# Attention projections from fp16 halves made by GpSimd, with the score scale moved into the queries' flips

## The chip, the core and the metric

The kernel runs as one program on one core of a Trainium2 chip. The metric is the device time of one execution in microseconds (us). The core's engines are PE (TensorE, matrix products; its weight loads are listed as PEld), DVE (VectorE), ACT (ScalarE), POOL (GpSimd) and the DMA queues, which SP (SyncE) and POOL issue to. Each engine runs its own list of instructions in order; they meet at semaphores.

## The reference, cut to what matters

One transformer block over x of 4 batches x 512 tokens x 128 channels: a normalisation with scale and shift, attention, a second normalisation, a mixture of eight experts. The part of attention that the change touches:

```
q = (x @ wq).reshape(B, N, H, D)       # B=4, N=512, H=16 heads, D=64
k = (x @ wk)                           # KV=4 heads, repeated to 16
v = (x @ wv)                           # KV=4 heads, repeated to 16
for n in range(K_NODES):               # 4 nodes; a token belongs to its top 2
    p = pos[..., n]                    # position of the token within node n
    qr = q * cos[p] + rotate_half(q) * sin[p]
    kr = k * cos[p] + rotate_half(k) * sin[p]
    scores = einsum('bhid,bhjd->bhij', qr, kr) * D ** -0.5
    scores = where(causal & member, scores, NEG)
    outs.append(einsum('bhij,bhjd->bhid', softmax(scores), v))
y = (tk_w * take(outs, tk_idx)).sum()
out = y @ wo
```

Everything is float32 in the reference.

## The kernel before, in words

The order of every engine's work is written out by hand. First comes a **preamble** (up to about 69 us): loads, first normalisation, `hT` (the normalised tokens, channels on the partitions, 128 x 2048), router scores, the choice of nodes and positions, and the first sines and cosines. Then comes the **attention loop**: 64 heads (4 batches x 16), numbered `n`, four steps `s` each (one block of 128 query rows), so k = 4n + s runs over 256 steps. Then comes the expert part with the output.

In the preamble SP loads the weights `wq` and `wk` into `w_qk` and `wv` into `w_v`; ACT multiplies the query weights by 0.125, which is the score scale (L557). DVE does the long chain that chooses nodes and positions (L807 to L894), POOL makes constants and two casts (L393).

For each head:
- `project(n)` on PE (L1184): four matmuls of float32, one for each block of 128 tokens, with 128 columns (64 of q, 64 of k), into the PSUM bank `psM`. `project_value(g)` (L1177) does four of 64 columns once for every four heads.
- `products(n, e)` on DVE (L905) multiplies them by cosines and sines, `rotate(n, part)` on POOL (L410 to L429) adds them up into `R` (queries in both slots) and `ktok`.
- `flip(i)` on PE turns a block of 128 tokens around: two transposes for the queries (L1228) and one for the keys (L1230), each through `ident`, a float32 identity. ACT copies the three results from PSUM to `QK` (L596, `keep_qk`).
- `scores(k)` on PE (L1243 to L1248), row maxima on DVE (L933, L940), exponentials on ACT (L617), coefficients on POOL (L436), the two weighted sums on ACT (L626) and DVE (L951), `prob_rows` on PE (L1257, one to four transposes), `values` (L1268) and every eight heads `attention_rows` (L1293).

PE's order in step k is: scores(k), flip(k+2), prob_rows(k-4), and in some steps values, project_value, attention_rows; in step s = 3 project(n+3) ends the step. A flip or prob_rows needs one of three PSUM banks in turn, so it waits until ACT has emptied the one used three turns before. DVE also makes the angles for later heads (L850 to L878) inside the loop, and once in eight heads ACT turns them into sines and cosines (L579, L580, with two table loads). POOL splits the experts' weights into float16 halves in step s = 1 of 48 heads (L449, L451).

## Time and profile before

| what | value |
|---|---|
| median of 3 runs | 980.61 us (980.22 to 987.98) |
| the profiled execution, its own time | 980.4 us |
| span from its first to its last instruction | 978.6 us |
| PE busy | 860.6 us, 88% of the span |
| DVE, ACT, POOL busy | 80%, 77%, 65% of the span |
| TensorE clock granted, mean | 0.965 of full speed |

The span is divided by reading the trace in stretches: the preamble ends with the first scores at 68.83 us, and the attention loop ends at 845.6 us. A profile's busy time of PE includes the modelled tail of each matmul, so the cost of one in a row of them is read from start to start. A float32 matmul appears in the trace as two instructions (x8 for the four of `project`), a float32 transpose and a float16 matmul as one.

### The profile page before, as it was taken

How to read it: one execution, taken by the hardware profiler on the slowest of the kernel's cores; microseconds unless marked ns; L12 is line 12 of the kernel's file. 1: busy time of each engine (PE TensorE's matmuls, PEld its weight loads, DVE VectorE, ACT ScalarE, POOL GpSimd, SP SyncE). 2: the span in 40 equal slices, each digit the busy share in tenths (PEclk: the TensorE clock that was granted, in tenths of full speed). 3: DMA queues.
4: the chain of work that ended last, by engine and by line, in shares of the span. 5: the costliest groups of instructions: out<-in, count | busy, mean ns of one | idle time of the engine just before them, and what ended most of it. 6: DMA issues, size and time to landing. Idle time of an engine off the chain costs nothing.

```text
span 978.6 us, 19653 instructions
## 1 busy us (share of the span) xinstructions
PE 860.6 (88%) x5960; PEld 610.1 (62%) x5960; DVE 787.0 (80%) x1832; ACT 753.6 (77%) x2032; POOL 632.5 (65%) x898
## 2 busy tenths in 40 slices
PE   4348979998999899989998999899989999998883
PEld 4336656666666665666666666666667676665773
DVE  4979979996999699969996999689967876686554
ACT  8427888788888888888788888888888887764552
POOL 1157767885878588857885788577856665036562
PEclk9659999999999999999999999999999999999997
DMA  9000001000100000100010000000000000324443
GB/s 223 13 0 8 13 12 33 26 24 12 28 29 27 11 24 27 32 13 23 24 34 13 24 24 28 20 24 24 19 2 2 3 2 10 111 76 135 116 127 103
DMA packets 54279, 36.65 MB, mean 37 GB/s; under 512 B 8384, under 2 KB 53056, under 8 KB 54176
## 3 DMA queue, kind: packets, MB, share of 16 engines
q1 hardware_dynamic: 52960, 32.88, 12.4%
q0 software_dynamic: 1216, 2.51, 0.8%
q8 instruction: 51, 0.84, 0.4%
q14 instruction: 52, 0.43, 0.1%
HBM read 22.23 MB, written 12.36 MB: 35 GB/s over the span
## 4 chain that ended last, share of the span: by engine, by line
PE 60%; DVE 26%; ACT 7%; issue 5%; POOL 1%; DMA 1%; DVEq 0%; ACTq 0%; POOLq 0%; SPq 0%
PE psum L1243 21%; PE psum L1268 7%; PE psum L1257 6%; PE psum L1184 5%; DVE pcs L905 4%; PE psum L1351 4%; PE psum L1228 4%; PE psum L1248 4%; DVE accs L951 3%; ACT probs L617 3%; DVE psum L940 3%; PE psum L1293 3%; DVE probs L1002 2%; DVE arena L878 2%; PE psum L1230 2%
## 5 line engine op out<-in xcount | busy, mean ns | idle before, releaser
L1243 PE MATMUL psum<-QK 128*128 128x128 f32 (+3 forms) x1024 | 375.4, 452 | 1.3 <-ACT QK L596 1.3
L617 ACT ACTIVATE probs<-psum,negmax 128x128 f32<-128x128 f32 (+3 forms) x512 | 266.5, 527 | 80.0 <-DVE negmax L940 48.1
L410 POOL TENSOR_TENSOR R<-pcs 128x512 f32<-128x512 f32 x128 | 190.5, 1509 | 64.9 <-DVE pcs L905 47.3
L940 DVE CUSTOM_DVE_ANT_0 psum<-psum,causal 128x384 f32<-128x384 f32 (+1 forms) x256 | 156.4, 637 | 57.8 <-PE psum L1248 57.6
L436 POOL TENSOR_TENSOR coef<-rden,wslot 128x2 f32<-128x2 f32 x256 | 87.2, 340 | 171.2 <-DVE rden L946 171.1
L1243 PEld LDWEIGHTS psum<-QK 128*128 128x128 f32 x1024 | 166.7, 195 | 45.7 <-issue 40.9
L951 DVE SCALAR_TENSOR_TENSOR accs<-probs,coef,accs 128x128 f32<-128x128 f32 (+3 forms) x256 | 169.2, 661 | 1.0 <-ACT accs L626 1.0
L626 ACT ACTIVATE accs<-probs,coef 128x128 f32<-128x128 f32 (+3 forms) x256 | 148.0, 578 | 23.3 <-POOL coef L436 23.3
L905 DVE TENSOR_TENSOR pcs<-psum,arena 128x512 f32<-128x512 f32 x256 | 161.7, 672 | 0.0
L1257 PE MATMUL psum<-ident,accs 128*128 128x128 f32 x640 | 116.3, 280 | 38.2 <-ACT QK L596 34.3
L596 ACT ACTIVATE QK<-psum 128x384 f32<-128x384 f32 x256 | 125.8, 491 | 1.9 <-PE psum L1230 1.8
L933 DVE TENSOR_REDUCE negmax<-psum 128x2 f32<-128x256 f32 (+1 forms) x128 | 70.5, 550 | 61.0 <-PE psum L1246 60.7
L605 ACT ACTIVATE arena<-psum 128x128 f32<-128x128 f32 (+3 forms) x256 | 114.6, 448 | 0.0
L1257 PEld LDWEIGHTS psum<-ident,accs 128*128 128x128 f32 x640 | 72.0, 141 | 62.9 <-issue 41.5
L617 ACT ACTIVATION_READ_ACCUMULATOR probs<-psum,negmax 128x1 f32 x512 | 102.8, 201 | 0.0
L1228 PE MATMUL psum<-ident,R 128*128 128x128 f32 x512 | 101.0, 279 | 1.3
L1184 PE MATMUL psum<-w_qk,hT 128*128 128x128 f32 x512 | 74.1, 291 | 30.1 <-DVE pcs L905 25.2
L1228 PEld LDWEIGHTS psum<-ident,R 128*128 128x128 f32 x512 | 59.7, 143 | 52.2 <-issue 42.0
L1248 PE MATMUL psum<-mring 128*128 128x384 f16 (+1 forms) x256 | 90.2, 352 | 0.0
L1184 PEld LDWEIGHTS psum<-w_qk,hT 128*128 128x128 f32 x512 | 67.0, 204 | 32.0 <-issue 18.9
L1268 PE MATMUL psum<-arena,v_b 128*64 128x256 f32 (+3 forms) x512 | 76.0, 439 | 0.9 <-ACT arena L605 0.7
L1230 PE MATMUL psum<-ident,ktoks 128*128 128x128 f32 x256 | 70.6, 276 | 0.0
(214 smaller groups left out, 1469.3 us busy)
## 6 DMA issues: line engine op xcount, KB each, us to landing
weight_halves<-whl SPq DMA_DIRECT2D x48, 128.0 KB, 2.2
arena<-weight_halves SPq DMA_DIRECT2D x22, 256.0 KB, 3.2
arena<-weight_halves SPq DMA_DIRECT2D x7, 512.0 KB, 6.9
wst<-in_L_ffn_w_up_dram SPq DMA_DIRECT2D x14, 128.0 KB, 2.5
wst<-in_L_ffn_w_gate_dram SPq DMA_DIRECT2D x14, 128.0 KB, 2.4
wst<-in_L_ffn_w_down_dram SPq DMA_DIRECT2D x14, 128.0 KB, 2.5
sorted_rows<-arena SPq DMA_DIRECT2D x1, 1430.0 KB, 11.4
QK<-sorted_rows SPq DMA_DIRECT2D x5, 260.0 KB, 3.9
```

Of the source, the lines that this page charges most:

```text
L410: pool.tensor_tensor(R[u][:, :, :, 0:3:2, half * HALF:(half + 1) * HALF].rearrange("p t e j f -> p (t e) j f"), halves(pc, half), halves(p ...
L617: act.activation((expB if e else expA)[:, k % (4 if e else 3), 0:w], area, ACT.Exp, scale=1.0 if k % TB < 2 else -1.0, bias=negmax[k % 4][ ...
L626: act.activation(acc[k % 4][:, 0:w], expA[:, k % 3, 0:w], ACT.Copy, scale=coef[k % 4][:, 0:1]).then_inc(S["wa_done"], 1)
L905: dve.tensor_tensor(dst[:, :, e, :].rearrange("p t (j f) -> p t j f", f=HALF), src, table.unsqueeze(2).to_broadcast([P, TB, 4, HALF]), ALU ...
L940: dve.tensor_tensor_reduce(score_area(k, e), score_area(k, e), causal[:, T - w:T], -1.0, 3e38, ALU.add, ALU.min, accum_out=negmax[k % 4][: ...
L951: dve.scalar_tensor_tensor(acc[k % 4][:, 0:w], expB[:, k % 4, 0:w], coef[k % 4][:, 1:2], acc[k % 4][:, 0:w], ALU.mult, ALU.add).then_inc(S ...
L1184: mm_ = pe.matmul(psM[:, tb * P:(tb + 1) * P], hT[:, b * T + tb * P:b * T + (tb + 1) * P], w_qk[:, h, :, :].rearrange("p j d -> p (j d)"), ...
L1228: pe.transpose(psT[:, e * P:(e + 1) * P], R[u][:, tb, e, 0:2, :].rearrange("p c d -> p (c d)"), ident[:, :])
L1243: pe.matmul(o, QK[:, u, e, rows], QK[:, u, 2, 0:w], start=True, stop=False)
L1248: mm_ = pe.matmul(o, mring[:, r, 1 + e, rows], mring[:, r, 0, 0:w], start=False, stop=True)
L1257: mm_ = pe.transpose(psPT[:, jb * P:(jb + 1) * P], acc[k % 4][:, jb * P:(jb + 1) * P], ident[:, :])
L1268: mm_ = pe.matmul(dst[u * HD:(u + 1) * HD, jb * P:T], v_b[:, p // 2 % 3, jb, :], accT[:, (2 * p + u) % 3, jb, jb * P:T], start=(jb == 0), ...
```

## The change

Attention's projections are made of float16 halves. A float32 value is kept as high = fp16(value) and low = fp16(value - high), and a product is the sum of three float16 matmuls (high x high, high x low, low x high) accumulated in PSUM. The helper `three`, which the expert part already has, is moved ahead and used in `project` and `project_value`. The weights `wq`, `wk`, `wv` are loaded as float32 into a part of `probs` that is still free; POOL splits them into `w_qk` and `w_v` (now float16, high and low), and then the tokens of batch 0 into a buffer that the router uses later. The tokens of batches 1 to 3 are split in the loop, 128 columns at a time, in step s = 3 of the heads n = 4 to 15, into the place of the `hT` of the batch before. PE waits for the halves (`hs_lo`). The query weights are no longer scaled. Instead the two query transposes of `flip` become plain float32 matmuls with `ident_q`, an identity times 0.125. The column of gates `gcol` is made by a copy instead of a multiplication with `ones`.

```
@@ -59,7 +59,7 @@
         ones16 = sb("ones16", [P, P], F16)
-        ones = sb("ones", [P, P])
+        ident_q = sb("ident_q", [P, P])
         half_pi = sb("half_pi", [P, 1])
@@ -71,8 +71,8 @@
-        w_qk = sb("w_qk", [P, H, 2, HD])
-        w_v = sb("w_v", [P, KV * HD])
+        w_qk = sb("w_qk", [P, 2, H, 2 * HD], F16)
+        w_v = sb("w_v", [P, 2, KV * HD], F16)
         w_r = sb("w_r", [P, H * NODES])
@@ -146,6 +146,9 @@
         w_mod = probs[:, :, :].rearrange("p g t -> p (g t)")[:, 0:6 * DIM]
+        w_qk32 = probs[:, :, :].rearrange("p g t -> p (g t)")[:, 1024:1024 + H * 2 * HD]
+        w_qk4 = w_qk32.rearrange("p (h j d) -> p h j d", j=2, d=HD)
+        w_v32 = probs[:, :, :].rearrange("p g t -> p (g t)")[:, 3072:3072 + KV * HD]
         xn = pcs_flat.rearrange("p (t d) -> p t d", d=DIM)
@@ -193,15 +196,20 @@
         passed = red_flat[:, 168:168 + SORTED * (E - 1)].rearrange("p (t e) -> p t e", e=E - 1)
-        rl = sb("rl", [P, NT, E])
-        rr = sb("rr", [P, 4, NT, E])
+        rbuf = sb("rbuf", [P, 4 * NT * E])
+        rl = rbuf[:, 0:NT * E].rearrange("p (t e) -> p t e", e=E)
+        rr = rbuf[:, NT * E:4 * NT * E].rearrange("p (k t e) -> p k t e", k=3, e=E)
         rm = sb("rm", [P, 4, NT])
-        one16 = rr[:, 3, :, :].rearrange("p t e -> p (t e)").bitcast(F16)[:, 0:(NT + 1) * E].rearrange(
-            "p (t e) -> p t e", e=E)
+        one16 = sb("one16", [P, NT + 1, E], F16)
+
+        def halves_of(b):
+
+            where = rbuf[:, 0:T] if b == 0 else hT[:, (b - 1) * T:b * T]
+            return where.bitcast(F16).rearrange("p (l t) -> p l t", l=2)
...
             mm_in0 mm_in1 mm_in2 c_exp c_sum c_rec c_silu mod_mm mod_raw mod_sign mod_mag mod_done
-            gcol_done ga_mm ga_ev wq_scaled bn_s bn_a var_e std_dev rs_step xn_done xn_a xn_t h_ready zeros_done big_done
+            gcol_done ga_mm ga_ev hs_hi hs_lo bn_s bn_a var_e std_dev rs_step xn_done xn_a xn_t h_ready zeros_done big_done
             lg_mm lg_ev rank_s rank_m w_tanh l_mem mem16 sel_a sel_b sel_cp code_p code_e gap_done
@@ -276,11 +284,11 @@
             sp.dma_start(w_r[:, :], wr).then_inc(S["wr_in"], 16)
-            sp.dma_start(w_qk[:, :, 0, :], wq.rearrange("p (h d) -> p h d", h=H)).then_inc(S["wr_in"], 16)
+            sp.dma_start(w_qk4[:, :, 0, :], wq.rearrange("p (h d) -> p h d", h=H)).then_inc(S["wr_in"], 16)
             for r in range(GROUP):
-                sp.dma_start(w_qk[:, r:H:GROUP, 1, :], wk.rearrange("p (g d) -> p g d", g=KV)
+                sp.dma_start(w_qk4[:, r:H:GROUP, 1, :], wk.rearrange("p (g d) -> p g d", g=KV)
                              ).then_inc(S["loaded"], 16)
-            for dst, src in ((freq[:, :], inv_freq), (w_v[:, :], wv),
+            for dst, src in ((freq[:, :], inv_freq), (w_v32, wv),
                              (w_o[:, :, :], wo.rearrange("(c p) n -> p c n", p=P)), (w_rt[:, :], w_router)):
@@ -359,12 +367,12 @@
             for t_, v in ((one_half, 0.5), (ident, 0.0), (ident16, 0.0), (identbig, 0.0), (causal, 0.0), (before, 1.0),
-                          (ones16, 1.0), (ones, 1.0), (half_pi, float(np.pi / 2))):
+                          (ones16, 1.0), (ident_q, 0.0), (half_pi, float(np.pi / 2))):
                 pool.memset(t_[:, :], v).then_inc(S["const_done"], 1)
...
             pool.wait_ge(S["const_done"], 11)
-            for t_, v in ((ident, 1.0), (ident16, 1.0), (identbig, BIG)):
+            for t_, v in ((ident, 1.0), (ident_q, HD ** -0.5), (ident16, 1.0), (identbig, BIG)):
                 pool.affine_select(out=t_[:, :], in_=t_[:, :], compare_op=ALU.not_equal, fill=v, base=0,
@@ -386,6 +394,19 @@
             pool.memset(floor8[:, E - 1:E], float(SORTED * P)).then_inc(S["ident_done"], 1)
+            def split_rows(i, high, low, src):
+                pool.tensor_copy(high, src).then_inc(S["hs_hi"], 1)
+                pool.wait_ge(S["hs_hi"], i + 1)
+                pool.tensor_tensor(low, src, high, ALU.subtract).then_inc(S["hs_lo"], 1)
+
+            pool.wait_ge(S["wr_in"], 32)
+            pool.wait_ge(S["loaded"], 16 * 8)
+            w_two = w_qk[:, :, :, :].rearrange("p l h c -> p l (h c)")
+            split_rows(0, w_two[:, 0, :], w_two[:, 1, :], w_qk32)
+            split_rows(1, w_v[:, 0, :], w_v[:, 1, :], w_v32)
+            pool.wait_ge(S["h_ready"], 1)
+            split_rows(2, halves_of(0)[:, 0, :], halves_of(0)[:, 1, :], hT[:, 0:T])
+            pool.wait_ge(S["lg_mm"], 2)
             pool.wait_ge(S["sel_a"], 4)
@@ -454,6 +475,10 @@
                     split(n - RING - 1)
+
+                if s == 3 and 4 <= n < 4 + (B - 1) * TB:
+                    b, cols = (n - 4) // TB + 1, slice((n - 4) % TB * P, (n - 4) % TB * P + P)
+                    split_rows(n - 1, halves_of(b)[:, 0, cols], halves_of(b)[:, 1, cols], hT[:, b * T:(b + 1) * T][:, cols])
                 m, part = (n + 2, s - 2) if s >= 2 else (n + 1, s + 2)
@@ -553,8 +578,6 @@
                 act.activation(lg[:, i * 512:(i + 1) * 512], bank[4 + i][:, :], ACT.Copy).then_inc(S["lg_ev"], 1)
-            act.wait_ge(S["wr_in"], 32)
-            act.activation(w_qk[:, :, 0, :], w_qk[:, :, 0, :], ACT.Copy, scale=HD ** -0.5).then_inc(S["wq_scaled"], 1)
             act.preload_act_table(ACT.Silu)
@@ -779,7 +802,7 @@
             dve.wait_ge(S["mod_raw"], 1)
-            dve.wait_ge(S["ident_done"], 7)
+            dve.wait_ge(S["ident_done"], 8)
             for j in range(2):
@@ -796,7 +819,7 @@
             for b in range(B):
-                dve.tensor_scalar(gcol[b], ones[:, :], mod[:, 2, b:b + 1], None, ALU.mult).then_inc(S["gcol_done"], 1)
+                dve.tensor_copy(gcol[b], mod[:, 2, b:b + 1].to_broadcast([P, P])).then_inc(S["gcol_done"], 1)
@@ -1141,7 +1164,7 @@
             mm_.then_inc(S["mod_mm"], 1)
-            pe.wait_ge(S["ident_done"], 7)
+            pe.wait_ge(S["ident_done"], 8)
@@ -1171,18 +1194,27 @@
+            def three(dst, w, x_, start, stop):
+                for j, (wl, xl) in enumerate(((0, 0), (0, 1), (1, 0))):
+                    mm_ = pe.matmul(dst, w[wl], x_[xl], start=start and j == 0, stop=stop and j == 2)
+                return mm_
+
+            def rows_of(b, tb):
+                return [halves_of(b)[:, l, tb * P:(tb + 1) * P] for l in range(2)]
+
             def project_value(g):
                 b = g // KV
+                pe.wait_ge(S["hs_lo"], 3 + TB * b)
                 for tb in range(TB):
-                    mm_ = pe.matmul(psM[:, tb * HD:(tb + 1) * HD], hT[:, b * T + tb * P:b * T + (tb + 1) * P],
-                                    w_v[:, (g % KV) * HD:(g % KV + 1) * HD], start=True, stop=True)
+                    mm_ = three(psM[:, tb * HD:(tb + 1) * HD], rows_of(b, tb),
+                                [w_v[:, l, (g % KV) * HD:(g % KV + 1) * HD] for l in range(2)], True, True)
                 mm_.then_inc(S["v_mm"], 1)
...
                 b, h = n // H, n % H
+                pe.wait_ge(S["hs_lo"], 3 + TB * b)
                 for tb in range(TB):
-                    mm_ = pe.matmul(psM[:, tb * P:(tb + 1) * P], hT[:, b * T + tb * P:b * T + (tb + 1) * P],
-                                    w_qk[:, h, :, :].rearrange("p j d -> p (j d)"), start=True, stop=True)
+                    mm_ = three(psM[:, tb * P:(tb + 1) * P], rows_of(b, tb), [w_qk[:, l, h, :] for l in range(2)], True, True)
                 mm_.then_inc(S["qk_mm"], 1)
@@ -1197,7 +1229,6 @@
                 mm_.then_inc(S["pos_mm"], 1)
-            pe.wait_ge(S["wq_scaled"], 1)
             pe.wait_ge(S["v_ev"], 1)
@@ -1225,8 +1256,9 @@
                 for e in range(2):
-                    pe.transpose(psT[:, e * P:(e + 1) * P], R[u][:, tb, e, 0:2, :].rearrange("p c d -> p (c d)"),
-                                 ident[:, :])
+
+                    pe.matmul(psT[:, e * P:(e + 1) * P], R[u][:, tb, e, 0:2, :].rearrange("p c d -> p (c d)"),
+                              ident_q[:, :], start=True, stop=True)
                 pe.transpose(psT[:, 2 * P:3 * P], ktok[u][:, tb, :, :].rearrange("p c d -> p (c d)"), ident[:, :]
@@ -1345,11 +1377,6 @@
                 mm_.then_inc(S["rank_mm"], 1)
-
-            def three(dst, w, x_, start, stop):
-                for j, (wl, xl) in enumerate(((0, 0), (0, 1), (1, 0))):
-                    mm_ = pe.matmul(dst, w[wl], x_[xl], start=start and j == 0, stop=stop and j == 2)
-                return mm_
...
                 if i >= 2:
```

**PE, the last projection of the preamble and the first flips**, before (`R` holds queries, `ktoks` keys):

```order
L1184 MATMUL psum<-w_qk,hT 128x128 [waits prod_done]
L1184 MATMUL psum<-w_qk,hT 128x128 x3
L1228 MATMUL psum<-ident,R 128x128 [waits k_done,q_done]
L1228 MATMUL psum<-ident,R 128x128
L1230 MATMUL psum<-ident,ktoks 128x128
L1228 MATMUL psum<-ident,R 128x128 [waits k_done,q_done]
L1228 MATMUL psum<-ident,R 128x128
L1230 MATMUL psum<-ident,ktoks 128x128
```

and in the changed kernel (`rbuf` holds the halves of batch 0's tokens):

```order
L1199 MATMUL psum<-w_qk,rbuf 128x128 [waits hs_lo,prod_done]
L1199 MATMUL psum<-w_qk,rbuf 128x128 x11
L1260 MATMUL psum<-ident_q,R 128x128 [waits k_done,q_done]
L1260 MATMUL psum<-ident_q,R 128x128
L1262 MATMUL psum<-ident,ktoks 128x128
L1260 MATMUL psum<-ident_q,R 128x128 [waits k_done,q_done]
L1260 MATMUL psum<-ident_q,R 128x128
L1262 MATMUL psum<-ident,ktoks 128x128
```

Each projection has 12 float16 matmuls where it had 4 of float32, with a wait on the halves; the flips stand where they stood, and two of the three are matmuls now.

**POOL, end of the constants to the first rotation**, before:

```order
L383 IOTA arena 128x22 [waits zeros_done,const_done]
L386 AFFINE_SELECT tri<-tri 128x64
L388 MEMSET floor 128x1
L393 CAST QK<-yT 128x1024 [waits sel_a]
L393 CAST QK<-yT 128x1024 [waits sel_b]
L410 TENSOR_TENSOR R<-pcs 128x8x2x32 [waits prod_done,codes_done]
```

and in the changed kernel:

```order
L391 IOTA arena 128x22 [waits zeros_done,const_done]
L394 AFFINE_SELECT tri<-tri 128x64
L396 MEMSET floor 128x1
L398 CAST w_qk<-probs 128x2048 [waits loaded,wr_in]
L400 TENSOR_TENSOR w_qk<-probs,w_qk 128x2048 [waits hs_hi]
L398 CAST w_v<-probs 128x256
L400 TENSOR_TENSOR w_v<-probs,w_v 128x256 [waits hs_hi]
L398 CAST rbuf<-hT 128x512 [waits h_ready]
L400 TENSOR_TENSOR rbuf<-hT,rbuf 128x512 [waits hs_hi]
L414 CAST QK<-yT 128x1024 [waits sel_a,lg_mm]
L414 CAST QK<-yT 128x1024 [waits sel_b]
L431 TENSOR_TENSOR R<-pcs 128x8x2x32 [waits prod_done,codes_done]
```

Six splitting instructions stand ahead of the two casts `QK<-yT`, for which PE waits (`sel_cp`).

**POOL, around step s = 3 of head n = 4** (`coef` are the coefficients that ACT waits for, `R` the next head's rotation), before:

```order
L410 TENSOR_TENSOR R<-pcs 128x8x2x32 [waits t_done,prod_done]
L410 TENSOR_TENSOR R<-pcs 128x8x2x32
L436 TENSOR_TENSOR coef<-rden,wslot 128x2 [waits rden_done]
L415 TENSOR_TENSOR R<-R,code 128x8x64 [waits add_done]
L418 TENSOR_TENSOR kdif<-R 128x256
L436 TENSOR_TENSOR coef<-rden,wslot 128x2 [waits rden_done]
```

and in the changed kernel:

```order
L431 TENSOR_TENSOR R<-pcs 128x8x2x32 [waits t_done,prod_done]
L431 TENSOR_TENSOR R<-pcs 128x8x2x32
L457 TENSOR_TENSOR coef<-rden,wslot 128x2 [waits rden_done]
L398 CAST hT<-hT 128x128
L400 TENSOR_TENSOR hT<-hT 128x128 [waits hs_hi]
L436 TENSOR_TENSOR R<-R,code 128x8x64 [waits add_done]
L439 TENSOR_TENSOR kdif<-R 128x256
L457 TENSOR_TENSOR coef<-rden,wslot 128x2 [waits rden_done]
```

A cast and a subtraction of 128 columns stand ahead of the second part of the next rotation and the coefficients after it; this occurs 12 times, in heads 4 to 15.

## Rows read from the trace of the kernel before

**Rows 1.** The chain that ended last, of the attention loop, by line.

```profile
by line: PE psum L1243 26.7%; PE psum L1268 8.9%; PE psum L1257 7.6%; PE psum L1184 5.7%; PE psum L1228 4.7%; DVE pcs L905 4.6%; PE psum L1248 4.4%; DVE accs L951 4.2%; ACT probs L617 4.2%; DVE psum L940 4.0%; issue 3.6%; PE psum L1293 3.2%
```

**Rows 2.** Busy us of eight heads on PE, PEld, DVE, ACT, POOL; then clock, DMA.

```profile
264.21:362.95 98.74, 93.61 (x578) 64.53 (x577) 84.62 (x194) 82.80 (x236) 73.91 (x105) 0.98 0.08 24
```

**Rows 3.** Timeline of PE at full clock: start us, us, line.

```profile
407.86 0.38 PE L1228 MATMUL psum<-ident,R 128*128 128x128 f32 x2
408.07 0.27 PE L1230 MATMUL psum<-ident,ktoks 128*128 128x128 f32 x1
408.18 0.60 PE L1257 MATMUL psum<-ident,accs 128*128 128x128 f32 x4
408.62 1.06 PE L1184 MATMUL psum<-w_qk,hT 128*128 128x128 f32 x8
409.51 0.39 PE L1243 MATMUL psum<-QK 128*128 128x128 f32 x2
```

**Rows 4.** The groups of PE by shape: busy us, mean ns of one.

```profile
L1169 PE MATMUL psum<-ident,kdif 128*128 128x128 f32 x4 | 0.7, 288 | 0.0
```

**Rows 5.** The chain of 264 to 363 us, in order of time: start, us, what.

```profile
271.68 2.14 DVE arena L878
...
274.60 1.45 ACT probs L617 x4
...
278.75 0.41 PE psum L1257 x2
...
346.25 0.84 PE psum L1177 x8
```

**Rows 6.** The waits of the whole span: us in total, times, longest us.

```profile
PE psum L1257 <- ACT QK L596: 34.3, 33, 3.5
```

**Rows 7.** Timeline of PE in the expert part: float16 matmuls in a row.

```profile
906.31 1.50 PE L1351 MATMUL psum<-mk,arena 128*128 128x128 f16 x24
907.65 0.90 PE L1397 MATMUL psum<-ident,QK 128*128 128x128 f32 x6
```

**Rows 8.** The chain of the preamble, in order of time.

```profile
22.94 3.25 DVE arena L807 x6
...
65.54 2.07 PE psum L1184 x8
67.61 0.43 PE psum L1228 x2
```

**Rows 9.** DMA issues: KB each, median us from issue to landing.

```profile
w_rt<-in_L_ffn_w_router_dram SPq DMA_DIRECT2D x1, 4.0 KB, 4.4
```

**Rows 10.** The groups of POOL by shape: busy us, mean ns of one.

```profile
L451 POOL TENSOR_TENSOR whl<-wst,whl 128x256 f16<-128x256 f32 x48 | 32.3, 673 | 3.8
L449 POOL CAST whl<-wst 128x256 f16<-128x256 f32 x48 | 19.0, 396 | 0.0
```

**Rows 11.** Timeline of the preamble: last load, PE, POOL's casts, DVE's angles.

```profile
11.96 0.58 SPq L285 DMA_DIRECT2D w_rt<-in_L_ffn_w_router_dram  x1
...
31.09 0.21 PE L1196 MATMUL psum<-arena,before 128*128 128x64 f16 x1 [3.25 <-DVE arena L819]
...
32.85 3.07 POOL L393 CAST QK<-yT 128x1024 f16<-128x1024 f32 x2 [21.05 <-DVE yT L827]
...
38.91 1.29 DVE L850 TENSOR_TENSOR arena<-slot,freq 128x512 f32<-128x512 f32 x2
...
42.82 0.46 DVE L873 TENSOR_SCALAR arena<-arena 128x576 f32<-128x576 f32 x1
...
53.35 2.34 DVE L850 TENSOR_TENSOR arena<-slot,freq 128x512 f32<-128x512 f32 x2
...
60.67 0.76 DVE L873 TENSOR_SCALAR arena<-arena 128x576 f32<-128x576 f32 x1
```

**Rows 12.** Busy us and timeline of PE after a long wait.

```profile
325.90:329.20 3.30, 3.30 (x17) 3.17 (x18) 0.00 (x0) 2.16 (x7) 0.00 (x0) 0.50 0.00 0
...
325.87 2.04 PE L1184 MATMUL psum<-w_qk,hT 128*128 128x128 f32 x8 [0.51 <-DVE x L963]
```

## The prediction

> **What bounds the kernel now.** I read the chain of waits of the attention loop first, by line, then the busy times of eight heads, then PE's timeline from start to start. The chain [rows 1] is mostly PE's: of the loop's 776.8 us (68.83 to 845.6) the score products L1243 have 26.7%, the projections L1184 5.7% and the query flips L1228 4.7%; DVE and ACT lines have the smaller pieces. In eight heads PE is busy 93.61 of 98.74 us, DVE 84.62, ACT 82.80, POOL 73.91 [rows 2]. So PE is the nearest bound and DVE the next. The expert part from 845.6 us on keeps its instructions; I cost it at nothing.
>
> **The flips, the largest term.** At full clock two query transposes take 0.21 us from start to start (407.86 to 408.07), the key's takes 0.11 and four of L1257 take 0.44, so a float32 transpose costs 0.11 us. The four float32 matmuls of a projection take 0.89 us (408.62 to 409.51), so a matmul of the same shape costs 0.2225 [rows 3]. The change turns 512 transposes (64 heads x 4 blocks x 2) into such matmuls: 512 x 0.1125 = 57.6 us more work for PE. That an identity as second operand makes nothing cheaper is seen at L1169, two plain matmuls by `ident`, which the trace has as four instructions [rows 4].
>
> A page speaks of another ratio. The Trainium skill (TensorE: Matmul & The Clock Gate, Terms) says that transpose mode is four times faster for float32. The rows just named give a factor of two, and I go by them; what four would do is the last rival.
>
> Not all of this is on the path. The chain's share of L1228 is 4.7% of 776.8 = 36.5 us, which is 329 transposes of 0.111. The others lie beside DVE or ACT work: the chain of one stretch goes through an angle step of DVE (2.14 us), then four instructions of ACT's exponentials (1.45 us), and comes back to PE at 278.75 [rows 5]. PE waited 34.3 us in 33 such places for ACT's copy, up to 3.5 us each [rows 6]; the two or three flips in front of such a place add only 0.23 us each, and vanish in it. So on the path: 329 x 0.1125 = **+37.0 us**, as a floor; if no wait hid anything, 57.6.
>
> **The projections.** A float16 matmul of 128 columns takes (907.65 - 906.31) / 24 = 0.056 us [rows 7]. Three of them, 0.168, replace 0.2225: 0.0545 saved x 256 = 14.0 us of PE work, 24.5% of L1184. The chain has 5.7% of 776.8 = 44.3 us of that line [rows 1]; 24.5% of it is **-10.9 us**. The 16 value projections (64 columns) took 0.84 us for eight instructions [rows 5], 0.21 a matmul. The trace has no float16 one of this shape in a steady row; at 0.168 for three, like the wider one, it saves 0.042 x 64 = 2.7, at half that time 8. I take **-2.0**, since the wide one has the same weight load, and keep 0 and -8.
>
> **The flips that are hidden now.** These floors hold if every wait stays as long as it is. Some waits are shorter than what is put in front of them, and there the flip becomes the later one. Of the 57.6 - 37.0 = 20.6 us that lie beside other work I let a tenth come through: **+2.0**, bounds 0 and 20.6.
>
> **The preamble.** The last projection before the loop is on the chain at half clock: 2.07 us, of which 65.54 to 67.61 is its length; the first two flips take 0.43 us each for their pair [rows 8]. The projection gets shorter by a quarter, -0.5, the two flips by 0.43 longer each, +0.9: **+0.4**. ACT's scaling of the query weights goes; it stood beside the chain of DVE, which runs without a hole from 22.94 us, so it gives nothing.
>
> POOL's splitting is new there. It starts when the last load has landed: `w_rt` is issued at 11.96 [rows 11] and takes 4.4 us [rows 9], so 16.4. The work per 256 columns is 0.396 for the cast and 0.673 for the subtraction [rows 10]. The query and key weights are 2048 columns: 8 x (0.396 + 0.673) = 8.6; the value weights 1.1; the tokens of batch 0 (512) 2.1. In all 11.8 us, to 28.2. Queued behind it are the two casts that POOL began at 32.85 us before, when DVE's selection is there [rows 11]; 4.6 us of cover. `project_value(0)` now waits for it on PE, and behind that stands L1196, which waits for DVE until 31.09 [rows 11]: 12 matmuls at half clock are 1.3 us, so it is done at 29.5, with 1.6 us of cover. If POOL took 3 us longer, 1.4 us would come onto the path.
>
> What it does cost is DVE's speed. The first five angle steps take 3.91 us to the start of L873 with POOL idle (38.91 to 42.82), and 7.32 us next to POOL's rotations (53.35 to 60.67) [rows 11], 1.87 times as long. DVE's chain starts at 22.94 [rows 8] and POOL works until 28.2: 5.3 us in which DVE gets 1/1.87 done, a loss of 2.4. I take **+2.4**, bounds 0 (these operands are not disturbed) and 5 (POOL is slowed too and stays until 33).
>
> **POOL in the loop.** Twelve times a cast and a subtraction of 128 columns, half of the above: 0.53 us, 6.4 in all. Behind them stand the next rotation and the coefficients for which ACT waits. POOL is idle for 98.74 - 73.91 = 24.8 us in eight heads [rows 2], mostly waiting for DVE; I take **+0.8** of the 6.4, bounds 0 and 6.4. The `gcol` copies and the 0.3 us for one more identity lie beside other work.
>
> **The sum.** The profiled execution's own time is 980.4 us (span 978.6), and the median of the runs 980.61, so the same sum serves both. 980.4 + 37.0 - 10.9 - 2.0 + 2.0 + 0.4 + 2.4 + 0.8 = 1010.1. I forecast **1010 us**, 3% slower. With the bounds of the parts that case reaches from 1000 to 1030.
>
> **The rivals.**
>
> *The clock stays up.* After PE's wait for ACT's sines and cosines the granted clock is half (1.2 GHz) for a while: 0.50 in 325.9 to 329.2, with PE busy throughout, and the projection there takes 2.04 us instead of 1.06 [rows 3, 12]. Six of the eight stretches of eight heads have a mean of 0.98 like [rows 2]. Each costs 3.3/2 = 1.65 us; if the flips, being matmuls, kept the clock at its upper level, 6 x 1.65 = 10 us would come back: 1000 us. Against it: what the clock fell after is a wait of about 2 us, and that wait stays. The Trainium skill (TensorE: Matmul & The Clock Gate, Part 4: PE-mode transpose) says that full clock does not engage for transposes as it does for matmuls; here it was full in a loop with 22 transposes a head (8 and 4 of the flips, 10 of L1257), so the trace does not bear it out. Chance 0.08.
>
> *Nothing is hidden.* If PE's waits follow its own work (the other engines are released later by the same amount), all of it counts: 980.4 + 57.6 - 14.0 - 2.7 + 0.4 + 2.4 + 0.8 = 1025 us, and with POOL at its bounds 1030. For it: PE is at 95% in eight heads. Against it: DVE and ACT stand in the chain with four lines of 4.0 to 4.6% among the twelve shown [rows 1]. Chance 0.11, inside the range.
>
> *The waits swallow it.* PE has 5.1 us without work in eight heads [rows 2], and the change adds 64 x 0.1125 - 32 x 0.0545 - 8 x 0.042 = 5.1. If DVE's and ACT's work were the true bound, the time would stay at 980.4 + 3.6 = 984 us. It decides at each wait: the added work before it must be shorter than it. The 33 waits are lumped in a few steps of each eight heads, and the chain crosses PE in between, so I give 0.05.
>
> *Faster: the flips cost what they did.* If a matmul by `ident_q` ran at the 0.11 us of a transpose, only the savings would be left: 980.4 - 10.9 - 2.0 + 2.4 + 0.8 - 0.5 = 970 us. It decides where 329 flips cost 10.2 us more, which is at 0.141 us each: below that the kernel gains. Two matmuls by `ident` [rows 4] speak against it. Chance 0.03.
>
> *Slower by far: a flip's matmul costs four transposes,* 0.44 us. On the path stand then 329 x 0.33 = 108.6 us instead of 37.0, which gives 1082 us. The steady row [rows 3] speaks against it: a projection's matmul has the same shape and type. Chance 0.01.
>
> **How the numbers follow.** A difference under 1% (9.8 us) can't be told from none here. The forecast has 0.72, the clock 0.08, nothing hidden 0.11, swallowed 0.05, faster 0.03, four transposes 0.01. Slower by over 1% are the forecast, the clock's case, the unhidden one and the last: 0.92; within 1% is the swallowed one, 0.05; faster 0.03. The range leaves out the last three and the ends of the bounds: 997 to 1027.
>
> **What the changed profile would show.** The flip line has 1024 instructions on PE, and two pairs take 0.44 us from start to start; 512 and 0.21 would mean the last rival. The projection line has 768 instructions, 12 in about 0.67 us. Eight heads in the middle take 98.7 + 3 to 4 us. The first scores start at about 71.5 instead of 68.83, with L807's six taking over 3.25 us. From the last scores to the end it stays at about 133 us. The prediction is wrong if the eight-head stretch grows by less than 1.5 us or more than 6, or if POOL's halves come after 31 us and hold PE.

## The result and the profile after

The changed kernel takes 990.11 us (median of 20 runs, 988.24 to 992.12), the kernel before 980.27 us (20 runs, 978.09 to 987.98): a ratio of 1.0086, 95% interval 1.0070 to 1.0102. It is slower, as forecast, but by 9.8 us and not by 30.

The profiled execution took 990.06 us for a span of 988.3 us. Cut at the first and the last score product, as the timeline of PE has them (start, us, line), the kernel before is

```profile
68.83 0.79 PE L1243 MATMUL psum<-QK 128*128 128x128 f32 x2
...
845.63 0.38 PE L1248 MATMUL psum<-mring 128*128 128x512 f16 x1
```

and the changed one

```profile
70.77 0.63 PE L1275 MATMUL psum<-QK 128*128 128x128 f32 x2
...
855.80 0.38 PE L1280 MATMUL psum<-mring 128*128 128x512 f16 x1
```

So the preamble is 1.9 us longer, the loop 8.2 us (785.0 instead of 776.8), and the rest of the span shrinks by 0.5. Below, "loop" is always taken to the start of the last score product: 776.4 us before, 784.6 after.

The chain that ended last, of the loop, by line, answers [rows 1]:

```profile
by line: PE psum L1275 26.7%; PE psum L1260 10.2%; PE psum L1300 8.8%; PE psum L1289 6.6%; PE psum L1199 4.9%; issue 4.5%; DVE pcs L928 4.2%; PE psum L1280 4.2%; DVE accs L974 3.0%; ACT probs L640 3.0%; PE psum L1262 2.3%; DVE psum L963 2.2
```

The flips (L1260) went from 4.7 to 10.2%, 43 us more, in a loop that grew by 8. What gave way stands in the same row: DVE's `accs` from 4.2 to 3.0%, ACT's `probs` from 4.2 to 3.0%, DVE's `psum` from 4.0 to 2.2%, the projections (L1199) from 5.7 to 4.9%.

Eight heads and the next eight (busy us of PE, PEld, DVE, ACT, POOL; clock), to [rows 2]:

```profile
270.57:368.75 98.18, 94.94 (x683) 69.68 (x681) 84.74 (x195) 82.68 (x236) 73.96 (x106) 1.00 0.08 24
368.75:468.51 99.76, 96.49 (x683) 71.11 (x681) 84.80 (x194) 82.80 (x236) 74.09 (x105) 0.98 0.08 23
```

Before, such a stretch took 98.74 with a clock of 0.98 [rows 2]. The first here took less, without any half-clock stretch, and the second 1.0 more. DVE, ACT and POOL have the same busy time as before.

PE's timeline at full clock, to [rows 3]:

```profile
414.19 0.61 PE L1260 MATMUL psum<-ident_q,R 128*128 128x128 f32 x4
414.64 0.27 PE L1262 MATMUL psum<-ident,ktoks 128*128 128x128 f32 x1
414.75 0.60 PE L1289 MATMUL psum<-ident,accs 128*128 128x128 f32 x4
415.18 0.83 PE L1199 MATMUL psum<-w_qk,hT 128*128 128x128 f16 x12
415.85 0.44 PE L1275 MATMUL psum<-QK 128*128 128x128 f32 x2
```

The pair of flips takes 0.45 from start to start (predicted 0.44) in four instructions, the projection 0.67 (predicted 0.67). But in the first two steps of each head, behind the short mask product L1278, the pair takes 0.50:

```profile
416.57 0.22 PE L1278 MATMUL psum<-causal,identbig 128*128 128x128 f16 x1
416.63 0.66 PE L1260 MATMUL psum<-ident_q,R 128*128 128x128 f32 x4
417.13 0.27 PE L1262 MATMUL psum<-ident,ktoks 128*128 128x128 f32 x1
```

Added up over the 256 flips of the trace, the query pairs take 58.9 us before and 124.5 after: 65.6 us more PE work, where the prediction reckoned with 57.6.

PE's waits for ACT's copy of the flips, to [rows 6]:

```profile
PE psum L1289 <- ACT QK L619: 22.0, 19, 3.0
```

That is 12.3 us and 14 places fewer than before. A part of the added flips went into this wait.

### The profile page after: what moved, and what is told of

It reads as the page before. It is cut to its first block, busy times and chain, and to the rows that moved or that the text cites. A ratio compares the mean times of both kernels' runs of the same rounds, so it can differ in the third digit from the quotient of the medians.

```text
span 988.3 us, 21417 instructions
## 1 busy us (share of the span) xinstructions
PE 882.8 (89%) x6792; PEld 659.3 (67%) x6792; DVE 789.6 (80%) x1832; ACT 753.1 (76%) x2031; POOL 651.6 (66%) x929
## 3 DMA queue, kind: packets, MB, share of 16 engines
q1 hardware_dynamic: 52960, 32.88, 12.2%
## 4 chain that ended last, share of the span: by engine, by line
PE 60%; DVE 21%; ACT 10%; issue 5%; POOL 2%; DMA 1%; DVEq 0%; ACTq 0%; POOLq 0%; SPq 0%
PE psum L1275 21%; PE psum L1260 8%; PE psum L1199 8%; PE psum L1300 7%; PE psum L1289 5%; DVE pcs L928 4%; PE psum L1280 3%; DVE accs L974 2%; ACT probs L640 2%; DVE probs L1025 2%; PE psum L1262 2%; DVE psum L963 2%; DVE arena L901 2%; PE psum L1277 2%; ACT arena L602 1%
## 5 line engine op out<-in xcount | busy, mean ns | idle before, releaser
L1260 PEld LDWEIGHTS psum<-ident_q,R 128*128 128x128 f32 x1024 | 144.4, 195 | 41.3 <-issue 37.3
L1260 PE MATMUL psum<-ident_q,R 128*128 128x128 f32 x1024 | 166.5, 286 | 0.5
L1289 PE MATMUL psum<-ident,accs 128*128 128x128 f32 x640 | 113.3, 275 | 23.4 <-ACT QK L619 22.0
L1289 PEld LDWEIGHTS psum<-ident,accs 128*128 128x128 f32 x640 | 76.4, 141 | 31.7 <-DVE accs L974 22.5
L436 POOL TENSOR_TENSOR R<-R,code 128x512 f32<-128x512 f32 x64 | 69.2, 1081 | 0.2
L1277 PE MATMUL psum<-mring 128*128 128x128 f16 (+1 forms) x256 | 63.9, 249 | 0.0
## 6 DMA issues: line engine op xcount, KB each, us to landing
sorted_rows<-arena SPq DMA_DIRECT2D x1, 1430.0 KB, 10.9
```

Of the source, the lines that this page charges most:

```text
L1260: pe.matmul(psT[:, e * P:(e + 1) * P], R[u][:, tb, e, 0:2, :].rearrange("p c d -> p (c d)"), ident_q[:, :], start=True, stop=True)
L1289: mm_ = pe.transpose(psPT[:, jb * P:(jb + 1) * P], acc[k % 4][:, jb * P:(jb + 1) * P], ident[:, :])
```

## The experiments

Each run stands beside executions of the kernel before on the same chip; the first four ran on one where the expert part takes 16 us longer for every kernel, so times are compared as ratios and by loop length. Unless said otherwise, an edit is to the kernel before. The loop length is that of the profiled execution alone, which isn't always near the median. In e4, e9, e10 and e12 PE's 32 products with `w_r`, ahead of the loop, took 7.06 us in it instead of 3.87, for a reason that stays open. In e5 (991.96 us) it is the fastest of five, in e8 (987.14 us) too.

| run | what it is | median us | ratio (95%) | loop us, from 776.4 |
|---|---|---|---|---|
| (after) | the change | 990.11 | 1.0086 (1.0070-1.0102) | 784.6, +8.2 |
| e1, e12 | projections changed, flips not | 993.51, 978.11 | 0.9947 (0.9927-0.9967), 0.9957 (0.9938-0.9976) | 772.4, -4.0; 775.5, -0.9 |
| e2 | flips changed, projections not | 1015.89 | 1.0160 (1.0121-1.0199) | 793.7, +17.3 |
| e3 | query transposes twice | 1006.47 | 1.0084 (1.0057-1.0111) | 785.2, +8.8 |
| e4 | change, and key flips as matmuls | 1019.70 | 1.0203 (1.0166-1.0241) | 797.6, +21.2 |
| e5 | 512 transposes behind the wait | 996.49 | 1.0154 (1.0117-1.0191) | 786.9, +10.5 |
| e6 | change, weights split early | 995.14 | 1.0146 (1.0115-1.0177) | 782.5, +6.1 |
| e7 | e1, weights split early | 983.63 | 1.0030 (1.0008-1.0051) | 771.9, -4.5 |
| e8 | change, no splits in the loop | 988.51 | 1.0079 (1.0045-1.0112) | 781.4, +5.0 |
| e9 | more DVE work, first step | 1018.19 | 1.0346 (1.0306-1.0386) | 812.5, +36.1 |
| e10 | more ACT work | 987.40 | 1.0066 (1.0043-1.0088) | 783.2, +6.8 |
| e11 | e1, splits in step s = 0 | 978.88 | 0.9975 (0.9955-0.9996) | 773.7, -2.7 |
| e13 | less DVE work | 972.12 | 0.9927 (0.9892-0.9963) | 766.3, -10.1 |
| e14 | change, less DVE work | 983.11 | 1.0001 (0.9977-1.0024) | 776.0, -0.4 |
| e15 | e9 and e3 together | 1023.74 | 1.0426 (1.0381-1.0472) | 819.0, +42.6 |
| e16 | DVE work behind the products | 1012.84 | 1.0311 (1.0274-1.0348) | 808.1, +31.7 |
| e17 | DVE work, second step | 1005.63 | 1.0247 (1.0206-1.0288) | 801.0, +24.6 |
| e18 | DVE work, fourth step | 1004.26 | 1.0204 (1.0158-1.0251) | 800.8, +24.4 |

### The parts of the change (e1, e2, e12)

e1, in the changed kernel:

```
-            ACT.Copy).then_inc(S["t_ev"], 1)
+            ACT.Copy, scale=HD ** -0.25).then_inc(S["t_ev"], 1)
...
-                    pe.matmul(psT[:, e * P:(e + 1) * P], R[u]..., ident_q[:, :], start=True, stop=True)
+                    pe.transpose(psT[:, e * P:(e + 1) * P], R[u]..., ident[:, :])
```

> The changed kernel, but the query flips are float32 transposes by the plain identity again, and the score scale is applied by ACT's copy of queries and keys from PSUM (factor 64^-0.25 on both). Only the float16 projections and POOL's splitting are left. Theory 1 (PE's work counts where PE has no waits): 57.6 us of PE work leave the changed kernel, of which some 26 us were beside waits; 990 - 28 = 962 to 972 us, against before -10 to -18. Theory 2 (waits hide PE's work in both directions, the loop is set by DVE and ACT): 978 to 986 us, hardly faster than before. In both, the first scores start at about 70.3 us, since POOL's splitting still runs beside DVE's ranking.

e2, in the kernel before, takes only the flips and drops ACT's scaling of the query weights:

```
-                    pe.transpose(psT[:, e * P:(e + 1) * P], R[u]..., ident[:, :])
+                    pe.matmul(psT[:, e * P:(e + 1) * P], R[u]..., ident_q[:, :], start=True, stop=True)
```

> The kernel before with the query flips as float32 matmuls by an identity times 0.125 and without ACT's scaling of the weights; projections in float32 as before. PE gets 57.6 us more work and saves nothing. The prediction's theory (the chain is a floor): 980 + 37 + 0.9 + 2 = 1020 us. Theory 1 (as measured in eight heads of the changed kernel, some 3.7 us of added PE work vanish in waits): 8 x (7.2 - 3.7) = 28, 1008 us. Theory 2: below 1000 us. If it is 1008 or more, the projections gave back far more than the 13 us of the prediction.

The flips as matmuls cost the loop 17.3 us with float32 projections and 784.6 - 772.4 = 12.2 us with float16 ones, for about 65 us more PE work. The projections give 4.0 (with POOL's splits of the loop in the same kernel) and 793.7 - 784.6 = 9.1. No PE work counts in full, neither added nor removed. e12 repeated e1's kernel on another chip. The ratio held; the loop was 3.1 us longer than e1's, so the 12.2 above is 9.1 by e12:

> The version with transposes in the flips and the scale in ACT's copy once more, on the chip of the three before it, so that the step of the splittings can be judged. A ratio to before of 0.993 to 0.997 as on the other chip, loop 772 us, first scores at 69.8 us.

### The clock, and the place of the added work (e3, e4, e5)

e3 doubles the query transposes (`for again in range(2)` around them): nearly the PE time of the matmul flips, but no matmuls.

> The kernel before with each query transpose done twice into the same place: PE gets the same 57.6 us more work, but as transposes. If only the length of the added work counts, the time is that of the matmul flips alone within 3 us. If plain matmuls keep the granted clock up where transposes don't (the rival on the clock), this one is 5 to 10 us slower than that and shows six stretches at the lower clock in the loop, the other fewer.

> The changed kernel with the key flip as a float32 matmul too: 256 x 0.1125 = 28.8 us more PE work. Theory 1: the waits of PE are nearly used up (4.3 us without work in eight heads of 98.2 to 99.8 us), so most of it counts: 990 + 20 to 28 = 1010 to 1018 us. If half vanishes again as in the change itself, 1000 to 1006.

The loop of e3 is 8.5 us shorter than that of e2, where 3 were expected at most, and the intervals of their ratios don't touch. Most of it is PE work after all: the doubled transposes take 114.0 us of the loop's 256 flips, the matmul pairs of e2 123.3, 9.3 more. The weight loads of these matmuls take 193 ns on the mean, those of the transposes 141.

On the clock, the count of half-clock stretches in the loop of each profiled execution speaks: 6 before, 4 after and in e2, 2 in e3 and in e4, 1 in e5. Transposes reduced them at least as well as matmuls, so the flips' kind isn't what keeps the clock up; of the runs with added PE work alone, every one has fewer. A stretch costs about 1.6 us (99.76 - 98.18 in the windows above).

e5 puts 512 transposes behind the wait for ACT's copy instead of in front of it:

```
-                for jb in range(ib + 1):
+                for jb in list(range(ib + 1)) + [ib, ib]:
```

> The kernel before with two more float32 transposes in every step, the last block of the probabilities turned three times instead of once, so behind PE's wait for ACT's copy and not in front of it; the flips are untouched. The added PE work is 512 x 0.107 = 55 us, as with the query transposes done twice, whose loop got 8.8 us longer than before's 776.4. Theory 1a (the wait in front of the probabilities' transposes swallows what stands right ahead of it): here the work stands behind it, and the loop grows by 25 to 45 us. Theory 1b (any slack of PE in the loop takes it, wherever it stands): the loop grows by 6 to 14 us.

The loop of the profiled execution grew by 10.5 us, against 8.8 for as many transposes in front of the wait. The other four executions of e5 took 4.3 to 5.6 us longer than that one, and the ratios (1.0154 against 1.0084) lie 7 us apart; no trace shows where those 4 us lie. So the place matters by 2 to 7 us. But the 25 to 45 us that should have come if the flips hid only because they stand before a wait did not come. The wait itself shrank here too, from 34.3 to 24.7 us. What takes the added work in is slack that PE has in many places. Most of it isn't in the view of waits. PE's timeline before:

```profile
400.00 0.39 PE L1228 MATMUL psum<-ident,R 128*128 128x128 f32 x2
400.23 0.27 PE L1230 MATMUL psum<-ident,ktoks 128*128 128x128 f32 x1
400.62 0.41 PE L1257 MATMUL psum<-ident,accs 128*128 128x128 f32 x2
```

L1230 is followed by L1257 after 0.39 us, though its price in a row is 0.11: 0.28 us of waiting, and the row shows no idle time, since the profile counts the modelled tail of each matmul as busy. With each instruction of heads 8 to 55 charged its price in a row, PE's own work before is about 86 of 98.4 us per eight heads: 12.4 us of slack, where busy time shows 5.1. About 1.4 of it is what the half-clock stretches cost. The same sum gives about 90 of 99.2 after, 93 of 99.3 in e3, 94 of 100.7 in e4. Added work comes through to 0.16 (e3), 0.2 (e5, profiled execution), 0.27 (e2), and the last 28.8 us, e4 over the change, to 0.45. This fits a slack that gets dearer as it is used up, though only e4 shows the last step.

### Which engine sets the loop (e9, e10, e13 to e18)

If not PE, then DVE? e9 repeats one DVE multiplication of `products`, ahead of the step's own two, in 56 heads; e10 repeats ACT's copy of the flips in every second block.

```
+                if n >= SPAN and e == 0:
...
+                    dve.tensor_tensor(spare..., src, again..., ALU.mult).then_inc(S["spared"], 1)
                 for i, dst in ((1, pc), (0, ps)):
```

> The kernel before with one more multiplication of DVE in each head from 8 on (the first of the products once more, into a spare tile nobody reads): 56 x 0.62 = 35 us more DVE work, PE's work as before. Theory 1 (PE is the bound, DVE stands second): the loop grows by less than 10 us over 776.4. Theory 2 (the loop is set by the hand-overs of DVE, ACT and PE together, and PE's own length counts for a fifth of what is added): DVE's work counts for half or more, 18 to 35 us.

> The kernel before with a second copy by ACT of every other flip from head 8 on, ahead of the copy that PE waits for, into a spare tile: 112 x 0.37 = 41 us more ACT work. Theory 1 (PE is the bound): the loop grows by less than 12 us. Theory 2 (hand-overs): ACT's copy stands straight in the path of scores and of the probabilities' transposes, 20 to 41 us.

DVE's busy time in the loop grew by 41.7 us and the loop by 36.1; ACT's grew by 37.4 and the loop by 6.8. PE's waits in e9, and then in e1, where PE's work had gone down instead:

```profile
PE psum L1263 <- ACT QK L597: 65.8, 82, 3.5
```

```profile
PE psum L1289 <- ACT QK L619: 45.4, 41, 3.5
```

34.3 us before [rows 6] became 65.8 with more DVE work and 45.4 with less PE work: PE's wait grows when the others take longer or PE less. I took this as "DVE sets the loop". e13 leaves out one multiplication of the second step in 56 heads (the output changes), e14 does so in the changed kernel:

```
+                    if n >= SPAN and e == 1 and i == 0:
+                        continue
```

> The kernel before with less work for DVE: from head 8 on, the 56 heads' second of the two row-code products (the 0.62 us multiplication for e = 1) is left out, about 35 us of DVE's loop work; the output changes. Theory (DVE sets the loop's length, though it is busy for 85% of it and PE for 95%): the loop shrinks by 20 to 35 us, ratio to the kernel before 0.965 to 0.98. Rival (DVE's load matters only upward, since PE with its 86 us of work in 98 us is next in line at once): the loop shrinks by under 10 us, ratio above 0.99.

> The changed kernel with the same 56 multiplications of DVE left out; the output changes. Theory (the flips' 57 us of PE work were hidden behind DVE): with DVE shorter PE comes to the fore, and the loop is 15 to 30 us longer than in the run before this one, where with DVE's full work the difference was 8.2 us. Rival (the loop passes on a fixed fifth of PE's added work, whatever DVE does): the difference stays at 6 to 11 us.

> The kernel before with DVE's extra multiplication (the run that lengthened the loop by 36 us) and with each query transposed twice (by itself 8.8 us). Theory (DVE sets the length, PE's extra 57 us hide behind it, all the more as DVE is now longer): the loop grows by at most 4 us over the 812.5 us of the run with DVE's extra work alone, ratio 1.033 to 1.040. Rival (each engine adds its share independently): it grows by 8 us or more, ratio 1.043 or above.

The theory fell. 36.2 us less DVE busy time gave back 10.1 us only, the change cost 776.0 - 766.3 = 9.7 us with a shorter DVE, hardly more than 8.2, and with a longer one the doubled transposes still cost 6.5 (8.8 without). Busy us of eight heads in e13 (heads 16 to 23, as above):

```profile
261.68:358.98 97.30, 93.10 (x579) 64.14 (x578) 80.09 (x186) 82.38 (x236) 73.84 (x105) 0.98 0.08 24
```

DVE has 4.5 us less than in [rows 2], the stretch is 1.4 shorter, and no engine is full. The last three put e9's extra work behind the products of the same step (e16), ahead of those of the second step (e17), and into a step without products (e18):

> The kernel before with the extra multiplication of DVE (0.62 us in each of 56 heads, some 35 us in all) in the same step of the head as in the run that cost 36 us, but behind that step's two products instead of ahead of them. Theory now (the loop is a ring of hand-overs, and what counts is whether the added time stands on the ring: the head's products, which POOL and PE's flips of the next head wait for): the loop grows by clearly less, 8 to 25 us. Rival (DVE is at its limit, any work comes through): 30 to 40 us, wherever it stands.

> The same extra multiplication ahead of the products of the head's second step, whose end is what POOL and the next head's flips wait for. Theory: here it stands on the ring most plainly, 25 to 40 us. Rival by the leave-out run (35 us less of DVE's work in this same step gave back 10): added work costs what left-out work gives, about 10 us.

> The kernel before with an extra DVE multiplication of 128 x 512 float32 from and to the core's memory, in the fourth step of each head from the 7th on (56 heads), behind that step's row maxima and sums and ahead of its share of the angles. Theory: no product stands behind it in that step, so the loop grows by 5 to 15 us. Rival (DVE at its limit): 30 us or more.

Neither side was right. Per us of added DVE busy time the loop grew by 0.87 (e9), 0.76 (e16), 0.75 (e17) and 0.72 (e18, where POOL's busy time grew by 21 us too): the place matters a little, and added DVE time comes through at seven tenths or more anywhere. Part of e18's is the clock's: its loop has 44 us at half clock, where the kernel before has 20, and the one of its four executions with a higher mean clock (0.963 instead of 0.954) took 998.65 us, the others 1003.59 to 1004.93. What is shown: at this point the loop passes on 0.7 to 0.9 of added DVE time, 0.2 of added ACT time, 0.15 to 0.45 of added PE time, and gives back only 0.28 of DVE time taken away. What the next limit is when DVE gets shorter stays open; it isn't PE's amount of work (e14), and no run lowered POOL's or ACT's beside a shorter DVE.

### POOL's splitting (e6, e7, e8, e11)

e6 (change) and e7 (e1) load the value weights before the others and start POOL's splitting on a semaphore of their own, 2.5 us earlier:

```
-            pool.wait_ge(S["loaded"], 16 * 8)
+            pool.wait_ge(S["wkv_in"], 16 * 5)
```

> The changed kernel with the value weights loaded right behind the key weights and a semaphore of their own for these five loads, so that POOL splits the weights from about 13 us on instead of 16.5 and is done with the tokens of batch 0 near the start of DVE's ranking at 22.8 us. If POOL's work beside the ranking is what made it slow (six instructions 5.10 us instead of 3.23), the first scores start 1.0 to 1.9 us earlier than at 70.8 us and the time falls by as much. If the slowness has another cause, nothing changes.

> The version with transposes in the flips and the scale in ACT's copy, with the early splitting added. The two gains should add: 0.9947 of before and 1 to 1.9 us less, so a ratio of 0.993 to 0.994 and first scores at 68.0 to 68.8 us. If POOL's work beside DVE did not matter, 0.9947 again.

The loop hardly changed (2.1 us shorter in e6, 0.5 in e7), the preamble grew by 6.7 us in e6 and 6.6 in e7. The timeline of e6, POOL and DVE:

```profile
14.01 1.96 POOL L399 CAST w_qk<-probs 128x2048 f16<-128x2048 f32 x1 [2.21 <-DMA probs<-in_L_attn_wv_dram]
16.05 4.05 POOL L401 TENSOR_TENSOR w_qk<-probs,w_qk 128x2048 f16<-128x2048 f32 x1
...
13.62 9.45 DVE L798 TENSOR_SCALAR pcs<-x,mv,rs 128x128 f32<-128x128 f32 x8
```

and DVE's row of the kernel before, and POOL and DVE of the changed kernel:

```profile
13.62 2.13 DVE L774 TENSOR_SCALAR pcs<-x,mv,rs 128x128 f32<-128x128 f32 x8
```

```profile
16.47 1.89 POOL L398 CAST w_qk<-probs 128x2048 f16<-128x2048 f32 x1 [4.67 <-DMA w_rt<-in_L_ffn_w_router_dram]
18.44 4.09 POOL L400 TENSOR_TENSOR w_qk<-probs,w_qk 128x2048 f16<-128x2048 f32 x1
...
25.00 1.41 POOL L400 TENSOR_TENSOR rbuf<-hT,rbuf 128x512 f16<-128x512 f32 x1
...
22.82 5.10 DVE L830 TENSOR_TENSOR arena<-accs 128x256 f32<-128x256 f32 x6 [6.53 <-ACT accs L580]
```

Eight DVE instructions of 2.13 us in all took 9.45 beside POOL's splitting, whose two long instructions end at 20.10. The longest single one (durations in ns, least/median/most) took 4.22 us instead of 0.34, as long as POOL's subtraction:

```profile
L798 DVE TENSOR_SCALAR pcs<-x,mv,rs x8: 343/730/4221, 13.6 to 21.8; 128x128 f32<-128x128 f32 x8
```

In the change POOL's two long instructions fell between 16.5 and 22.5, where DVE waits anyway (6.53 us idle in its row), and only the small splits met the ranking: 5.10 us instead of 3.25 [rows 8]. In e12 the ranking started at 26.12 (after the longer `w_r` products), behind the splitting, and took 3.24.

e8 leaves out the splits in the loop and uses batch 0's halves for all batches (the output changes); e11 moves them to step s = 0 of the same heads.

> The changed kernel without the twelve splittings in the loop; the projections of batches 1 to 3 use the halves of batch 0, so this part of the computation is changed, and the work of PE, DVE and ACT stays. If POOL's 12 x about 0.5 us delay coefficients and rotations, the loop is 2 to 4 us shorter than the changed kernel's 784.6 us, above all in heads 8 to 15 (101.4 us there, 98.2 to 99.8 in later eights). If POOL's idle time hides them, less than 1 us.

> The version with transposes in the flips and the scale in ACT's copy, with the twelve splittings of POOL moved from step 3 to step 0 of the same heads, where POOL has one short rotation instead of two long ones. Leaving them out shortened the changed kernel's loop by 3.2 us. If their place makes that cost, the loop is 1 to 3 us shorter than that version's 772.4 us, mostly in heads 8 to 15, and the ratio to before 0.992 to 0.994; if POOL is short of time in every step, no difference.

Leaving them out saves 784.6 - 781.4 = 3.2 us of the loop, where I had 0.8. By the ratios (1.0086 and 1.0079) it is only 0.7 us, so the two can't be told apart. Elsewhere in the head the splits cost the same (773.7 us against 772.4 and 775.5 in e1's kernel).

## Why the prediction was right in sign and wrong in size

- **The step that failed** is the flips on the path, "**+37.0 us**, as a floor", with "These floors hold if every wait stays as long as it is". The price of a pair in a row was right to 0.01 us; with the pairs of 0.50 the added work was 65.6 us, which should have cost more and not less. The waits did not stay: PE's waits for ACT's copy fell from 34.3 to 22.0 us, and the hidden ones inside busy time shrank as well. The term measured +17.3 (e2), or +12.2 and +9.1 (the change over e1 and e12). The chain had 36.5 us of L1228 before, and that share was no floor: after the change it shows 43 us more of the line and 8 us more of time. The likely reason, argued and not shown by itself, is that the chain names one path where others are nearly as long: when a piece of PE's gets longer, waits of PE elsewhere get shorter. The sum had no lower value for this term, so with every other term at its low bound it still gives 999 us. (All bounds together reach from 999 to 1039, not from 1000 to 1030 as written.)
- **PE as "the nearest bound"** was read from 93.61 busy of 98.74. PE's own work was about 86 of 98.4, and a us more of DVE costs three to five times what a us of PE costs. "The waits swallow it" (0.05) compared the added 5.1 us per eight heads with 5.1 us of slack seen and 12.4 there; it comes nearest at 984, and the true 990 lies between it and the forecast, outside the range from 997.
- **The projections**, -10.9 and -2.0, together -12.9: measured -4.0 (e1) and -0.9 (e12), both with POOL's splits of the loop, and -9.1 beside the new flips. They gave less than forecast, by the same step: the chain's share was taken for what a change of the line is worth.
- **Hidden flips coming through**, +2.0, can't be told apart from the rest; with +37.0 refuted as a floor it has no meaning of its own.
- **The preamble** +0.4 and +2.4 and POOL beside DVE: measured +1.9 together, the ranking 1.85 longer, forecast 2.4. POOL was done at 26.41, not 28.2: one cast of 2048 columns took 1.89 us (3.2 estimated from 256-column ones), the subtraction 4.09 (5.4).
- **POOL in the loop**, +0.8: 3.2 by the loop of e8, 0.7 by its ratio, both inside the bounds.
- **The clock's rival** named a gain that exists in part (6 stretches became 4, about 3 us in the profiled execution), by a cause that e3 refutes: transposes did it as well.
- **Nothing is hidden, faster, four transposes**: the first is refuted by the loop's +8.2, the other two by the 0.45 to 0.50 us of a pair of flips, where they needed at most 0.28 and about 0.88.

The best version is e1's: float16 projections, transposes kept, the score scale split evenly over queries and keys in ACT's copy, where it costs no instruction. By the ratios it beats the kernel before by 0.4 to 0.5% and the change by 1.3%.

## What to carry to other kernels

A line's share of the chain is neither a floor nor a price: cost an added instruction by what the engine's start-to-start timeline leaves free, and do the sum per engine. In a loop of hand-overs tuned until several engines are at 85 to 95%, each has its own rate of coming through; two runs, one with more work on an engine and one with less, measure it, and the two can differ threefold. A scale that has to go somewhere belongs into a copy that exists, not into an instruction that it makes dearer.

## What the runs showed of the hardware

- A single-source float32 operation of DVE can last as long as the POOL instruction beside it: 4.22 us instead of 0.34 beside a subtraction of 4.05 (e6). Eight of them, 2.13 us in all, took 9.45 (e6) and 8.32 (e7). Products of two sources from the core's memory went from 3.25 to 5.10 in the change, beside POOL instructions of 0.4 to 1.4 us; as these were short, the two kinds can't be compared.
- Two float32 matmuls by an identity took 0.45 us in one place and 0.50 behind a short float16 product, where two transposes take 0.22 in both.
- PE's busy time hides waits: a gap of 0.28 us stood in rows without any idle time.
- POOL's long instructions are cheaper by column: a cast to float16 took 0.92 ns per column at 2048 columns and 1.55 at 256 (0.396 us [rows 10]), a subtraction 2.0 and 2.6.
- More work for PE of either kind, transposes or matmuls, meant fewer half-clock stretches in the loop: 6 before, 4 in e2, 2 in e3, 1 in e5, in one profiled execution each.
